# Attention's row maxima: each product of a block on its own 64 rows of TensorE's array

## What is computed

```
q = query.reshape(N, Q, HEADS, HEAD_DIM)          # 16 heads of 16
energy = jnp.einsum('nqhd,nkhd->nhqk', q, k)
energy = jnp.where(mask == 0, jnp.float32(-1e+20), energy)
attn = jax.nn.softmax(energy / jnp.sqrt(jnp.float32(EMB)), axis=-1)
out = jnp.einsum('nhqk,nkhd->nqhd', attn, v).reshape(N, Q, EMB)
return out @ W_out.T
```

## Time and profile before

| | us |
|---|---|
| median of three runs | 808.2 |
| the three runs | 807.15 to 808.49 |
| the profiled execution | 807.73 |
| its span, first to last instruction | 805.9 |
| TensorE busy in the span | 688.0 |
| VectorE busy | 626.8 |
| ScalarE busy | 502.6 |
| GpSimd busy | 313.7 |
| mean granted clock of TensorE | 0.941 of full |

### The profile page before, as it was taken

How to read it: one execution, slowest core, us unless ns; L and a number is a source line. 1 busy time by engine, 2 the same in 40 slices (tenths; PEclk the granted TensorE clock), 3 DMA queues, 4 the chain that set the end, 5 groups by cost and what they waited for, 6 DMA issues and landing times.

```text
span 805.9 us, 11812 instructions
## 1 busy us (share of the span) xinstructions
PE 688.0 (85%) x4157; PEld 528.1 (66%) x4157; DVE 626.8 (78%) x1210; ACT 502.6 (62%) x682; POOL 313.7 (39%) x250
## 2 busy tenths in 40 slices
PE   6882059999999788999999999999999999009998
PEld 5761037988888654556656656577887888007998
DVE  5998867787786488887676685988888899997654
ACT  2235614445553346796887887666655998896873
POOL 4354612667777444242431420003430444693000
PEclk9996559999999999999999999999999999559999
DMA  9937633566534650010023000004210834101443
GB/s 294 326 106 261 209 86 119 143 174 161 144 61 53 151 197 1 2 48 27 1 74 105 9 19 27 27 27 157 105 52 3 291 125 157 52 0 53 131 132 105
DMA packets 59541, 84.97 MB, mean 105 GB/s; under 512 B 7904, under 2 KB 47712, under 8 KB 57952
## 3 DMA queue, kind: packets, MB, share of 16 engines
q1 hardware_dynamic: 49936, 61.10, 22.8%
q0 software_dynamic: 7872, 21.11, 10.8%
q10 hardware_dynamic: 1680, 2.08, 0.7%
HBM read 53.74 MB, written 30.54 MB: 105 GB/s over the span
## 4 chain that ended last, share of the span: by engine, by line
PE 57%; DVE 15%; ACT 11%; issue 4%; POOL 3%; DMA 1%; POOLq 0%; ACTq 0%; DVEq 0%
PE bank L2387 11%; PE bank L2181 8%; PE bank L2125 7%; PE bank L2411 5%; PE bank L1472 4%; PE bank L1506 3%; PE bank L1529 3%; PE bank L1566 3%; PE bank L1526 3%; DVE above L796 2%; PE bank L1487 2%; PE bank L1510 2%; ACT wgateT L2074 1%; DVE high L1907 1%; POOL wupT L1794 1%
## 5 line engine op out<-in xcount | busy, mean ns | idle before, releaser
L1329 ACT ACTIVATE x<-bank,bic 128x512 f32<-128x512 f32 x160 | 106.2, 697 | 35.1 <-PE bank L1506 33.7
L1203 DVE TENSOR_REDUCE qx<-bank 128x4 fp32r<-128x616 f32 x128 | 98.3, 797 | 28.0 <-PE bank L1472 26.5
L2125 PE MATMUL bank<-ux,uwh 128*128 128x512 f32 x384 | 95.7, 390 | 0.2 <-ACT ux L2019 0.2
L2125 PEld LDWEIGHTS bank<-ux,uwh 128*128 128x128 f32 x384 | 71.9, 188 | 15.7 <-issue 0.6
L1506 PE MATMUL bank<-qT,K 128*128 128x512 f32 x128 | 61.8, 493 | 3.5 <-ACT x L1329 2.0
L2348 ACT ACTIVATE wgateT<-bank 128x512 f32<-128x512 f32 x32 | 19.2, 599 | 65.5 <-PE bank L2387 65.5
L1472 PE MATMUL bank<-Kb,qTb 128*128 128x308 bf16 x256 | 53.7, 301 | 4.6 <-DVE qx L1203 2.0
L1130 POOL CAST qx<-q 128x1024 fp32r<-128x1024 f32 x8 | 8.5, 1068 | 114.2 <-PE bank L1487 105.2
L2125 PE MATMUL bank<-ux,uwl 128*128 128x512 f32 x192 | 51.4, 389 | 0.0
L2387 PE MATMUL bank<-xh,wh 128*128 128x512 f32 x128 | 50.0, 390 | 0.3 <-DVE xl L2321 0.3
L2387 PE MATMUL bank<-xl,wh 128*128 128x512 f32 x128 | 50.0, 390 | 0.0
(11 more groups left out here) (427 smaller groups left out, 2045.9 us busy)
## 6 DMA issues: line engine op xcount, KB each, us to landing
xs_dram<-ux POOLq DMA_DIRECT2D x6, 1024.0 KB, 4.3
ux<-xs_dram POOLq DMA_DIRECT2D x6, 1024.0 KB, 5.6
x_dram<-x SPq DMA_DIRECT2D x4, 1024.0 KB, 5.4
xr<-in_w1T SPq DMA_DIRECT2D x8, 512.0 KB, 3.9
xr<-in_w3T SPq DMA_DIRECT2D x8, 512.0 KB, 4.8
xr<-in_w2T SPq DMA_DIRECT2D x8, 512.0 KB, 6.4
row_dram<-xn SPq DMA_DIRECT2D x8, 512.0 KB, 3.0
x_dram<-xr SPq DMA_DIRECT2D x8, 512.0 KB, 2.9
```

Source lines behind the costliest of these rows:

```text
L1203: dve.tensor_reduce(qx[:, k, g * GH:(g + 1) * GH, MROW].rearrange("p (u h) -> p u h", u=2), pair[i][:].rearrange("p (u x) -> p u x", u=2)[ ...
L1329: act.activation(pr[g % 2][h], S_[u % 2], ACT.Exp, bias=bic[:, s // 2, h // GH:h // GH + 1]).then_inc(p_done, 1)
L2125: mm = pe.matmul(bank[j][:, m * TB:(m + 1) * TB], w[:, c * HI + cols:c * HI + cols + P], x[:, part, c * TB:(c + 1) * TB], start=(w is uwh ...
```

## The change

Product u of a block takes, of both operands, the 64 partitions that hold its two heads: partitions 0 to 63 for heads 0 and 1, 64 to 127 for heads 2 and 3. The rest of each operand was multiplied with zeros before. Where the products write, how many columns they stream, their order and their semaphores stay as they are; MW is 32. Everything behind the edited line moves down by one line in the source.

```
                     for u in range(2):
-                        mm = pe.matmul(dst[:, u * QN:u * QN + 2 * S2], qTb[:, k, g, :],
-                                       Kb[s // 2 % 2][:, g, u * 2:u * 2 + 2, :].rearrange("p h s -> p (h s)"), start=True, stop=True)
+                        rows = slice(u * 2 * MW, (u + 1) * 2 * MW)
+                        mm = pe.matmul(dst[:, u * QN:u * QN + 2 * S2], qTb[rows, k, g, :],
+                                       Kb[s // 2 % 2][rows, g, u * 2:u * 2 + 2, :].rearrange("p h s -> p (h s)"), start=True, stop=True)
                     mm.then_inc(sent, 1)
```

## The result

| | before | changed |
|---|---|---|
| median, runs side by side | 807.75 us | 817.21 us |
| ratio | | 1.0116, 95% interval 1.0098 to 1.0135 |
| ratio in a second comparison (6 runs against 18) | | 1.0086, 1.0063 to 1.0109 |
| profiled execution | 807.73 us | 818.38 us |

The change makes the kernel slower, by 9.4 us in the first comparison and 7.0 in the second. The predicted range was 809 to 821 and the forecast 814.5.

A forecast was written before the change was run, and what follows sets the result against it. TensorE was taken to bound attention's step, except a stretch bound by ScalarE. At +0.94 us a step, 6.5 steps give +6.1 and the first 24 blocks +0.4: +6.5 in all, so 814.5 us, range 809 to 821.

The forecast's parts named there:

- The bound: Attention step of 28.8 us: TensorE from 370.8 to 378.6, ScalarE to 389.5, then TensorE with VectorE close behind to 399.6.
- The overlap: In each block the two half-row products run side by side; the second costs 0.01 us instead of 0.13.
- Rival 2: Attention blocks: borders cost and the halves run one after the other, 8.6 us more, 823; chance 0.08.
- The borders: Attention: each change of shape costs, 0.11 us into a block and 0.20 out of it into a 32-bit product.
- Rival 1: Attention blocks: no border cost for 64 rows, only the overlap, so faster by 3.9 us, 804; chance 0.13.
- The sum of a step: One attention step: +1.65 us gross, +0.94 us after waits cover part; it should last 29.6 to 29.9 us.
- (a): Step from 370.8 to 378.6 us: two runs of blocks delay ScalarE's copy and the transposes; sum +0.33 us.
- (b): Step from 378.6 to 389.5 us: ScalarE is the bound and TensorE's waits cover the four runs; sum 0.
- (c): Step from 389.5 to 399.6 us: seven runs, exits cost 1.37 us, the blocks save 0.76; sum +0.61.
- The sum of attention: All of attention: +6.1 us for 104 blocks from 312 us on, +0.4 for the first 24; sum +6.5.
- The first 24 blocks: Start of attention, before 312 us: VectorE and ScalarE hold most of the chain; +0.4 us, ends 0 and +2.5.
- rival 4: Attention: an emptier array loses its clock more often; two or three further falls would make 818; chance 0.06.

The follow-up runs named there:

- rows_hidden: Changed kernel with only the five blocks of a step under ScalarE's cover on 64 rows, the other eleven as before; step 28.81 us, ratio to before 1.0034.
- rows_open: Changed kernel with only the eleven blocks of a step outside ScalarE's cover on 64 rows, the other five as before; step 29.64 us, ratio to before 1.0101.
- same_rows: Changed kernel with both products of a block on rows 0 to 63, so they can't run side by side; step 31.32 us, ratio to before 1.0234.
- scores_rows: Changed kernel with the 16 scores of a step also on 64 rows, result unchanged; step 30.00 us, ratio to before 1.0178.
- rows_pairs: Changed kernel with only the two runs of two blocks behind L1526 on 64 rows, four blocks a step; step 28.75 us, ratio to before 0.9995.
- before_delay_40: Kernel before with 40 more unread products at the end of attention, so later stages start later; 817.9 us beside 810.07 of before, one execution.
- before_delay_16: Kernel before with 16 more unread products at the end of attention, so later stages start later; 811.12 us beside 810.07 of before, one execution.

## Why the prediction was right, and where it was off

**The bound.** TensorE is the bound of the step but for the stretch under ScalarE: rows_hidden and rows_open show it, 0.0 and +0.82 us a step where the prediction had 0 and +0.94.

**The overlap.** Taken from four products on columns at 0.12 a block; it is 0.13 (same_rows). The row that the prediction cites, 0.99 against 0.87 us, gives 0.04 for each of three further products and not 0.01, unless the border into L1526 is taken out of it, which the prediction doesn't say; by its own price of 0.11 next to nothing is left, and next to nothing is what was measured. Rival 2, the halves one after the other, is out; had it been so, the time would be about that of same_rows, 829.5, and not the 823 that the prediction gave it. The price of that rival was too low, by the two blocks told above; same_rows also has a longer fall of the clock at 301 us than any other profile.

**The borders.** Taken as 0.11 in and 0.20 out, from the neighbours of L1526. They are 0.11 and 0.20, and scores_rows shows them on other neighbours. Rival 1, no border, is out. The 0.07 us between a load's start and the end of the product before it was the best sign in the trace: it stood at the border of columns, of one row, and now of 64 rows. The Trainium skill's rule on tiling modes ("TensorEngine Tiling (Array Packing)", Tiling Modes) holds here both ways: within the mode no price (a score behind a block in scores_rows, 0.23), across it a price each time.

**The sum of a step.** Predicted 29.6 to 29.9 us with +0.94 (its parts (a), (b) and (c) are those of the prediction), measured 29.67 with +0.85. By its stretches: ScalarE's copy of the turned queries starts 15.61 us into the step (388.07) and started 15.30 into it before, so (a) is +0.31 of a predicted 0.33. The score behind it is 0.31 late as well, so (b) is 0. (c) is +0.54, where I had 0.61: each of its seven runs takes 0.01 less than worked out.

**The sum of attention.** Predicted +6.5, measured 5.6 to 5.7 between the two first profiles, which both have one fall of the clock, at 309 to 310 us. By stretches: the 43 blocks up to the first product of L1566 at 341.7 cost 1.0, where the prediction's terms give 1.5 (0.4 and 19 blocks at 0.94/16); the five steps behind them cost 4.1, not 4.7 (the kernel before needs 28.96 for the first of them); the last five blocks 0.6, not 0.3. So the term that was too large is the price of a step, and that of the blocks before the full steps. (The first 24 blocks end at 319 us, not at 312.)

That comparison holds the falls of the clock equal, and the kernels don't. The kernel before has six profiles of attention, those with products added behind it among them: between 276 and 342 us three have no fall (attention takes 254.7 us) and three have one (255.7 to 255.9). Of the seven profiles with products on 64 rows none is without. The first of the changed kernel, rows_open and rows_pairs have one; the second of the changed kernel, rows_hidden and scores_rows have two; same_rows has one three times as long. Attention of the changed kernel takes 261.5 and 262.1 us, 5.6 to 7.4 more than before, in the mean 6.5. That this is the predicted number is luck: the sum had no falls in it. Whether products on 64 rows make such falls more frequent, which is rival 4, stays open with so few profiles; in the full steps the clock held at 1.00.

**Behind attention.** Here the prediction failed in a step of its own: "the stages before 276 and after 535 us should keep their lengths". Those before did (attention starts at 280.0 us before and at 279.9 after), those behind didn't. A fall of the clock at 624 us added about 1.1 net, behind a pause that the change moved by 5.6 us. Rival 4 looked for such falls in attention, because of an emptier array, and not in a stage that only starts later. 5.6 + 1.1 = 6.7 us is what the runs explain with equal falls in attention, and the second comparison measured 7.0. The first measured 9.4; its profile lost 3.9 more in the down projection, by a fall at 744 us and the slower pace. Since the slower pace also shows in before_delay_40 and in rows_pairs, whose edits are small or elsewhere, and such a fall in before_delay_16, I take both for chance. That it occurred in all of the first comparison's executions isn't known, as only one of them was profiled.

## What to carry to other kernels

In this kernel splitting the rows of the array pays when the products that share the split stand in a row. Each pair saves 0.13 us and each return to full rows costs 0.20, so a lone pair between two 32-bit products loses 0.18 and two pairs behind an existing border just win. Before restricting a product's rows or columns, count the changes of shape in TensorE's order, price each by the weight load that follows it, as it came out here, and look for a wait that covers it. A change that only delays a later stage may still change that stage's clock: compare stage by stage, count the falls of the clock in each, and profile the same kernel twice.

## What the runs showed of the hardware that I had not expected

A pause of TensorE of the same length (1.27 and 0.54 us) is followed by the lower clock level in some executions and not in others: at delays of 1.8 and 5.9 us yes, at 0, 3.6 and 9.1 no, and it costs the up projection 1.5 us each time. The same code of early attention ran with no fall in three profiles and with one in three. Identical streams of products on 256 columns run at a mean of 276 or of 281 ns and more, and the down projection takes 65.7 or 68.0 to 68.1 us without a fall of the clock, in different executions. I know no cause for it; the slower pace appeared in 4 of 13 profiles. And the loads of two halves of the rows run side by side, 0.10 us for both.
